# Last stage of an eight-sequence decoder: memory attention in chunks of 128 tokens with a carried state, one product for query and key, and the masked attention's shift per query by GpSimd and ScalarE

## What is computed

```
# memory attention (x: 8 x 512 x 256; M = 64; decay one number, 0.9 to 0.999)
q = x @ Wq; k = x @ Wk; v = x @ Wv; gates = sigmoid(x @ Wg + bg)
S = decay * S + (k_t*g_t)[:, None] * (v_t*g_t)[None, :]     # for t = 0, 1, ...
out_t = q_t @ S                                             # uses the new S
x = layernorm(x + (outs @ Wo + bo))
# masked attention to the context c
Q = x @ Wq.T + bq; K = c @ Wk.T + bk; V = c @ Wv.T + bv
attn = softmax(where(mask, -1e9, Q @ K.T))
x = layernorm(x + ((attn @ V) @ Wo.T + bo))
# experts: x @ expert_w[e] + expert_b[e], e = 0..7, weighted by thresholded softmax gates
```

## Time and profile before

| | |
|---|---|
| time, median of 3 runs | 2000.97 us (1998.99 to 2003.04) |
| the profiled execution's own time, its span | 1999.51 us, 1997.6 us |
| busy over the span: PE, PEld, DVE, ACT, POOL | 1829.3, 1077.1, 1250.3, 976.7, 614.7 us |
| mean granted TensorE clock, share of full speed | 0.970 |
| last stage | from 1377.6 us to the end |
| instructions | 26201 |

### The profile page before, as it was taken

How to read it: one execution, slowest core, us unless ns; L and a number is a source line. 1 busy time by engine, 2 the same in 40 slices (tenths; PEclk the granted TensorE clock), 3 DMA queues, 4 the chain that set the end, 5 groups by cost and what they waited for, 6 DMA issues and landing times. The chain is left out here.

```text
span 1997.6 us, 26201 instructions
## 1 busy us (share of the span) xinstructions
PE 1829.3 (92%) x8441; PEld 1077.1 (54%) x8441; DVE 1250.3 (63%) x2929; ACT 976.7 (49%) x2532; POOL 614.7 (31%) x795
## 2 busy tenths in 40 slices
PE   7999778899889888898879999998799999999997
PEld 5556434455444454454455566564466566556553
DVE  2686468888999989897302211322666776865665
ACT  4336599988989899895221111111233232222220
POOL 2010065555766666675400001002421212301100
PEclk9999989999999999999989999998889999999999
DMA  5348721122223122124633434423211111100000
GB/s 211 103 148 296 246 71 54 49 67 61 77 67 91 61 83 80 54 90 154 207 116 124 140 106 140 145 95 116 79 54 48 48 32 38 48 11 16 11 11 21
DMA packets 163800, 183.24 MB, mean 92 GB/s; under 512 B 19380, under 2 KB 143531, under 8 KB 162640
## 3 DMA queue, kind: packets, MB, share of 16 engines
q1 hardware_dynamic: 157520, 165.39, 25.9%
q0 software_dynamic: 6144, 16.18, 2.6%
HBM read 118.95 MB, written 63.18 MB: 91 GB/s over the span
## 5 line engine op out<-in xcount | busy, mean ns | idle before, releaser
L907 POOL TENSOR_SCALAR xa_probs<-xa_probs,xa_small 128x512 f32<-128x512 f32 x512 | 344.8, 690 | 244.8 <-DVE xa_small L1064 244.8
L973 ACT ACTIVATE xa_probs<-xa_ps_s,xa_small 128x512 f32<-128x512 f32 x512 | 361.1, 742 | 40.0 <-DVE xa_small L1070 36.1
L1070 DVE TENSOR_REDUCE xa_small<-xa_ps_s 128x2 f32<-128x1024 f32 x256 | 309.2, 1208 | 43.6 <-PE xa_ps_s L1341 43.6
L1354 PE MATMUL xa_ps_t<-xa_ident,xa_probs 128*128 128x128 f32 x2048 | 309.2, 284 | 17.0 <-DVE early L738 7.1
L1354 PEld LDWEIGHTS xa_ps_t<-xa_ident,xa_probs 128*128 128x128 f32 x2048 | 230.1, 143 | 153.3 <-ACT early L740 46.2
L2409 PE MATMUL ta_ps_e<-late,ta_x5T 128*128 128x512 f32 x512 | 236.9, 597 | 1.8 <-DVE ta_acc L2159 1.7
L1341 PE MATMUL xa_ps_s<-xa_k,xa_q 96*128 96x512 bf16 x496 | 152.3, 389 | 53.9 <-ACT xa_probs L973 53.9
L2159 DVE SCALAR_TENSOR_TENSOR ta_acc<-ta_ps_e,ta_gate,ta_acc 128x256 f32<-128x256 f32 x256 | 123.5, 482 | 95.0 <-PE ta_ps_e L2409 88.6
L1605 ACT ACTIVATE ex_hid<-ex_ps_g 128x512 f32<-128x512 f32 x64 | 38.2, 597 | 274.1 <-PE ex_ps_u L1702 274.1
L1656 DVE TENSOR_TENSOR ex_hid<-ex_hid,ex_ps_u 128x512 f32<-128x512 f32 x64 | 44.0, 688 | 185.1 <-ACT ex_hid L1605 185.1
L2409 PEld LDWEIGHTS ta_ps_e<-late,ta_x5T 128*128 128x128 f32 x512 | 96.4, 193 | 100.1 <-issue 83.7
(11 more groups left out here) (355 smaller groups left out, 3042.7 us busy)
## 6 DMA issues: line engine op xcount, KB each, us to landing
scratch_qk_parts<-front_w_all SPq DMA_DIRECT2D x16, 768.0 KB, 5.7
xa_q<-scratch_qk_parts SPq DMA_DIRECT2D x186, 64.0 KB, 2.3
xa_k<-scratch_qk_parts SPq DMA_DIRECT2D x186, 64.0 KB, 2.3
scratch_buf<-late SPq DMA_DIRECT2D x8, 1024.0 KB, 5.3
early<-in_L_ffn_Wg SPq DMA_DIRECT2D x16, 512.0 KB, 6.2
early<-in_L_ffn_Wu SPq DMA_DIRECT2D x16, 512.0 KB, 6.5
early<-in_L_ffn_Wd SPq DMA_DIRECT2D x16, 512.0 KB, 6.9
ex_xs<-scratch_buf SPq DMA_DIRECT2D x16, 512.0 KB, 5.2
```

The source lines that it names most:

```text
L907: ins = pool.tensor_scalar(probs[n % NP][:, t, :], probs[n % NP][:, t, :], rinv[n % 2][:, t:t + 1], 1.0, ALU.mult, ALU.mult)
L973: ins = act.activation(probs[n % NP][:, t, :], ps_s[j][:, t % 2, :], ACT.Exp, bias=nmax[n % 2][:, t:t + 1], accum_out=rsum[n % 2][:, t:t + 1])
L1070: dve.tensor_reduce(nmax[n % 2][:, 2 * j:2 * j + 2], ps_s[j][:, :, :], AX.X, ALU.max, negate=True).then_inc(max_up, 1)
L1354: ins = pe.transpose(ps_t[t % 2][:, i * P:(i + 1) * P], probs[m % NP][:, i, t * P:(t + 1) * P], ident[:, :])
```

## The change

**Memory attention.** The tokens are cut into four chunks of 128. Inside a chunk, scores and reading stay as they were (`m_scores`: four products of 128 columns into one buffer, `ps_a`; `m_faded`: one VectorE instruction of 512 columns). What earlier chunks leave is a 64 x 64 state: ScalarE makes `aged` (the keys times the decay to the end of the chunk, natural layout, 3 chunks), `m_outer` on TensorE multiplies it with the gated values, `m_carry` on VectorE chains the three states (state = whole * state + new), GpSimd makes `risen` (the queries times the decay since the chunk's start), and `m_reading` adds state times risen to the chunks 1 to 3. Query and key come from one product with the weights side by side (`m_qk`, 64 + 64 columns) in place of two padded ones, and the keys in natural layout come with the values (`m_vk`, 130 columns in place of 66 for three of the four tiles).

**Shift per query.** TensorE's `x_side` goes. GpSimd multiplies x4 by `cq_w`, now a row of 256 repeated over the partitions (`side`), and ScalarE sums each of the 4 tiles in an activation with an accumulator (`x_sides`).

**Stages before.** Fewer zero fills, one more weight load, one more small copy on GpSimd; the decay tables grow to 128 columns twice (`fade`, `rise`) in place of 512 once.

```diff
@@ gpsimd, stage_tail
                 if has(s_ - 1):
                     pool.wait_ge(m_x4, s_)
+                    wait(pool, x_cq, s_ - 1)
+                    pool.tensor_tensor(side[:, :, :], x4[(s_ - 1) % 2][:, :, :], row(cq_w[:, :]).to_broadcast([P, T, D]), ALU.mult).then_inc(x_side, 1)
                     wait(pool, x_z, T * (s_ - 1))
                     pool.tensor_tensor(x4b[:, :, :], ...).then_inc(m_x4b, 1)
+                if has(s_):
+                    pool.wait_ge(m_copy, 2 * s_ + 1)
+                    wait(pool, m_o, s_)
+                    pool.tensor_tensor(risen[:, :, :], qT[:, P:S].rearrange("p (t q) -> p t q", q=P),
+                                       row(rise[0:M, :]).to_broadcast([M, T - 1, P]), ALU.mult).then_inc(m_risen, 1)
@@ scalar
+                wait(act, m_kv, b)
+                act.activation(aged[:, :, :], ps_mkeys, ACT.Copy, scale=last).then_inc(m_aged, 1)
...
-            def x_side(b):
-                act.wait_ge(x_q, b + 1)
+            def x_sides(b):
+                act.wait_ge(x_side, b + 1)
+                for t in range(T):
+                    ins = act.activation(side[:, t, :], side[:, t, :], ACT.Copy, accum_out=cq_sum[:, t:t + 1])
+                ins.then_inc(x_sum, 1)
                 wait(act, x_ss, T * b)
-                act.activation(cq[:, :], ps_v[:, :, 0], ACT.Identity, bias=cq_b[:, 0:1]).then_inc(x_cq, 1)
+                act.wait_ge(x_sum, b + 1)
+                act.activation(cq[:, :], cq_sum[:, :], ACT.Identity, bias=cq_b[:, 0:1]).then_inc(x_cq, 1)
@@ vector
-            def m_faded(b, j):
-                dve.wait_ge(m_a, 4 * b + j + 1)
-                if j < 2:
-                    wait(dve, m_o, b)
-                else:
-                    dve.wait_ge(m_free, 2 * b + j - 1)
-                dve.tensor_tensor(aT[j % 2][:, 0:S - j * P], ps_s[j % 2][:, 0:S - j * P], fade[:, 0:S - j * P], ALU.mult).then_inc(m_at, 1)
+            def m_faded(b):
+                dve.wait_ge(m_a, b + 1)
+                wait(dve, m_o, b)
+                dve.tensor_tensor(aT[:, :, :], ps_a, row(fade[:, :]).to_broadcast([P, T, P]), ALU.mult).then_inc(m_at, 1)
+
+            def m_carry(b):
+                dve.wait_ge(m_kv, b + 1)
+                wait(dve, m_o, b)
+                dve.tensor_copy(state[:, 0, :], ps_kv[:, 0, :]).then_inc(m_state, 1)
+                for j in range(1, T - 1):
+                    dve.wait_ge(m_state, (T - 1) * b + j)
+                    dve.scalar_tensor_tensor(state[:, j, :], state[:, j - 1, :], whole[0:M, 0:1], ps_kv[:, j, :], ALU.mult, ALU.add).then_inc(m_state, 1)
@@ tensor
-                for n, w in enumerate((m_wq, m_wk)):
-                    for h in range(DH):
-                        ins = pe.matmul(ps_s[n][:, :], w[:, h, :], x3T[:, h, :], start=(h == 0), stop=(h == DH - 1))
-                    ins.then_inc(m_q, 1)
+                wait(pe, m_state, (T - 1) * b)
+                for h in range(DH):
+                    ins = pe.matmul(ps_s[0][:, :], m_qk[:, h, :], x3T[:, h, :], start=(h == 0), stop=(h == DH - 1))
+                ins.then_inc(m_q, 1)
...
+            def m_outer(b):
+                pe.wait_ge(m_aged, b + 1)
+                pe.wait_ge(m_gv, b + 1)
+                for t in range(T - 1):
+                    ins = pe.matmul(ps_kv[:, t, :], aged[:, t, :], gv[:, t, :], start=True, stop=True)
+                ins.then_inc(m_kv, 1)
+
+            def m_reading(b):
+                pe.wait_ge(m_at, b + 1)
+                pe.wait_ge(m_state, (T - 1) * (b + 1))
+                pe.wait_ge(m_risen, b + 1)
+                wait(pe, x_vs, 2 * b)
+                for t in range(T):
+                    ins = pe.matmul(ps_o[0:M, t * P:(t + 1) * P], gv[:, t, :], aT[:, t, :], start=True, stop=(t == 0))
+                    if t > 0:
+                        ins = pe.matmul(ps_o[0:M, t * P:(t + 1) * P], state[:, t - 1, :], risen[:, t - 1, :], start=False, stop=True)
+                ins.then_inc(m_o, 1)
...
-            def x_side(b):
-                wait(pe, m_gv, min(b + 2, B))
-                wait(pe, x_eT, T * b)
-                for t in range(T):
-                    for h in range(DH):
-                        ins = pe.matmul(ps_v[:, t, 0:2], x4T[:, h, t * P:(t + 1) * P], cq_w[:, h, :], start=(h == 0), stop=(h == DH - 1))
-                ins.then_inc(x_q, 1)
```

More of the change, by code:

```diff
@@ L582 @@
 M = 64
+W = 2 * M + 2
 MASKED = -1.0e9
@@ L602, in __init__ @@
         self.bq, self.bk, self.bv = (sb([P, DH]) for _ in range(3))
-        self.bqw, self.bvw = sb([P, DH, P]), sb([P, DH, P])
-        self.g_bias, self.cq_w, self.cq_b = sb([P, DH]), sb([P, DH, 2]), sb([P, 1])
+        self.bqw, self.bkw, self.bvw = (sb([P, DH, P]) for _ in range(3))
+        self.g_bias, self.cq_w, self.cq_b = sb([P, DH]), sb([P, D]), sb([P, 1])
         self.v_bias, self.bo = sb([P, D]), sb([P, D])
@@ L1646, in grow @@
                     dve.wait_ge(fade_up, 1)
-                wait(dve, grown, 2 * n)
-                dve.tensor_tensor(decay[:, n + 1:n + 2], decay[:, n:n + 1], decay[:, n:n + 1], ALU.mult).then_inc(grown, 1)
-                dve.tensor_scalar(k.fade[:, 1 << n:2 << n], k.fade[:, 0:1 << n], decay[:, n:n + 1], None, ALU.mult).then_inc(grown, 1)
+                    dve.wait_ge(decay_up, 2)
+                wait(dve, grown, 3 * n)
+                square = decay[:, n + 1:n + 2] if n + 1 < FADE else k.whole[:, :]
+                dve.tensor_tensor(square, decay[:, n:n + 1], decay[:, n:n + 1], ALU.mult).then_inc(grown, 1)
+                for row_ in (k.fade, k.rise):
+                    dve.tensor_scalar(row_[:, 1 << n:2 << n], row_[:, 0:1 << n], decay[:, n:n + 1], None, ALU.mult).then_inc(grown, 1)
             dve.wait_ge(sig_up, 1)
-            dve.tensor_scalar(decay[:, 0:1], sg[:, :], 0.999 - 0.9, 0.9, ALU.mult, ALU.add).then_inc(decay_up, 1)
+            for first in (decay[:, 0:1], k.rise[:, 0:1]):
+                dve.tensor_scalar(first, sg[:, :], 0.999 - 0.9, 0.9, ALU.mult, ALU.add).then_inc(decay_up, 1)
             for m in range(NU):
@@ L1753, in stage_tail @@
         z, z2 = r.sb("z", [P, T, D]), r.sb("z2", [P, T, D])
-        qT, kT, oT = (r.sb(n, [P, S]) for n in ("qT", "kT", "oT"))
+        qT, kT, oT = (r.sb(n, [M, S]) for n in ("qT", "kT", "oT"))
+        risen, state = r.sb("risen", [M, T - 1, P]), r.sb("state", [M, T - 1, M])
+        aged = r.sb("aged", [P, T - 1, M])
         g, g2 = r.sb("g", [P, T]), r.sb("g2", [P, T])
-        aT = [r.sb(f"aT{j}", [P, S]) for j in range(2)]
+        aT = r.sb("aT", [P, T, P])
         x4 = [r.sb(f"x4{u}", [P, T, D]) for u in range(2)]
@@ L1790, in stage_tail @@
         ps_o = r.ps("ps_o", [P, S])
+        line = ps_v[:, :, :].rearrange("p t q -> p (t q)")
+        ps_mv = [line[:, W * t:W * t + (W if t < T - 1 else M + 2)] for t in range(T)]
+        ps_mvalues = bass.AP(tensor=line.tensor, offset=0, ap=[[T * P, P], [W, T], [1, M]])
+        ps_mgates = line[:, M:M + W * (T - 1) + 1:W]
+        ps_mkeys = line[:, 0:W * (T - 1)].rearrange("p (t w) -> p t w", w=W)[:, :, M + 2:W]
+        ps_a = ps_s[1][:, :].rearrange("p (t q) -> p t q", q=P)
+        ps_kv = ps_s[0][0:M, 0:(T - 1) * M].rearrange("p (t m) -> p t m", m=M)
         ps_vx = ps_o[:, :].rearrange("p (t d) -> p t d", d=D)
@@ L1926, in x_turned @@
                 wait(act, x_g, b)
-                wait(act, x_q, b)
                 act.activation(x4T[:, :, :], ps_w[:, :, :], ACT.Copy).then_inc(x_xT, 1)
@@ L1984, in step @@
                 if has(b):
-                    x_side(b)
+                    x_sides(b)
                 if has(s_):
```

126 lines of the change are left out of this document (53 added, 73 removed).

## The result

The changed kernel takes 1976.29 us (median of four runs, 1975.09 to 1982.4) against 2002.01 us of the kernel before (four runs, 1998.99 to 2004.08): a ratio of 0.9886, 95% interval 0.9864 to 0.9907. It is faster, by 25.7 us between the medians and 24.2 us between the spans of the two profiled executions, and not by the 38 that I forecast; the time lies above my range, whose end was 1974.

What follows compares the result with a forecast made beforehand. The prediction took TensorE to bound the kernel. Its terms, −33.5 us in five full steps, −3 in steps 0 to 2 and −1.7 in step 8, made −38 from 2001.0, so 1963 us, range 1952 to 1974.

Steps and rivals of the forecast that it cites:

- 8 instructions for scores and 14 for readings at 0.108, 2.38 us: Full step, TensorE: with `m_outer` at 0.5 us these replace 5.97 us of scores and readings, −3.1 us a step.
- the floor of 0.108 us per instruction: TensorE: an instruction of up to 128 columns costs 0.108 us, read from products of 66 columns.
- Sum. −33.5: Steps 3 to 7: TensorE's savings of 6.7 us a step, over five full steps.
- my 64.9: Full step after the change: predicted length in us, so query and key products of steps 3 and 5 about 130 apart.
- the lower bound: Full step, six `m_outer` products: 0.32 us if load and columns both scale, half the upper bound of 0.65.
- Project, values, shift: Full step, TensorE: query and key in one product −1.72 us, values unchanged, `x_side` gone −1.89.
- The clock: Full steps: half clock behind the logits given back, 1.67 us a step; rival that it still falls: 1971 us, chance 0.16.
- The other engines in a full step: Full step: VectorE keeps 2.1 us of room, ScalarE's added work stays hidden with about 1 us; cost 0.
- Steps 0 to 2: First steps, chain over VectorE: 0 net for steps 0 and 1, −3 us for step 2.
- the sign of being wrong that I had named: Profile after: steps 0 to 2 longer than the 151 us they had by more than 2.
- one round fewer between TensorE and VectorE: Step 0: the carry needs one round where fadings 2 and 3 needed two, about 3 us, taken as 2.5.
- Step 8: Last step: `x_side` goes, 1.8 us there, taken as −1.7 us.

Runs made afterwards that it cites:

- full_tiles: Changed kernel with all memory-attention products padded by zeros to 128 rows and columns: 1967.54 us, ratio 0.984 to the kernel before.
- grouped: Changed kernel with the readings reordered, the four 128-row products first, then the three with the states: 1975.11 us, ratio 0.9887 to the kernel before.
- x_only: Kernel before with only the shift per query moved to GpSimd and ScalarE, memory attention as before: 1980.83 us, ratio 0.9915.
- m_only: Changed kernel with the shift per query back on TensorE as eight narrow products: 2010.31 us, ratio 1.0041 to the kernel before.
- gather_early: Changed kernel with GpSimd's gathers for the third batch right behind `risen` in step 0: 1978.31 us, ratio 0.9883 to the kernel before.
- late_mix: Changed kernel with VectorE combining the next batch behind the carry in steps 0 and 1: 1976.38 us, ratio 0.9881 to the kernel before.
- pool_later: Changed kernel with GpSimd doing `risen` first, then `side`, x3b and x4b once the next batch is combined: 1974.82 us, ratio 0.9885 to the kernel before.

## Why the prediction was wrong, point by point

**The step that failed** is "8 instructions for scores and 14 for readings at 0.108, 2.38 us", with the floor of 0.108 us per instruction taken to hold for any rows and columns, and "Sum. −33.5" from it. Measured: scores 1.09, readings 2.38, together 3.47 us, 1.1 more, and the neighbours that I had not counted: four units beside narrow products at 0.1 to 0.2 each, the output product 0.19, the transposition ahead of the scores 0.10, the logits 0.08: together 2.0 us a step, 4.66 for 6.7. Over five full steps that is 9.8 of the 14 us that are missing. full_tiles and grouped show the cause; full_tiles, whose step of 65.2 is near my 64.9, shows that the rest of the sum held. The trace of the kernel before had it (PE's timeline in step 4):
```profile
1631.12 0.60 PE L2394 MATMUL ta_ps_w<-late,ta_gate 128*8 128x128 f32 x4
1631.56 1.88 PE L2409 MATMUL ta_ps_e<-late,ta_x5T 128*128 128x512 f32 x4
1633.28 1.88 PE L2354 MATMUL ta_ps_s<-ta_cT,ta_gT 128*128 128x512 f32 x4
1635.09 1.99 PE L2400 MATMUL ta_ps_w<-late,ta_gateT 8*128 8x256 f32 x8
1637.01 1.98 PE L2354 MATMUL ta_ps_s<-ta_cT,ta_gT 128*128 128x512 f32 x4
1638.83 3.60 PE L2409 MATMUL ta_ps_e<-late,ta_x5T 128*128 128x512 f32 x8
```
The gate-bias product with 8 rows took 1.92 us for eight of 256 columns, where other eights of 256 take 1.73, and the products of 512 columns around it 1.81 and 1.82 for 1.72. I had not looked at products with few rows. One change costs nothing here, and in the same way after the change and in full_tiles: the transposition of the gates, with 128 rows and 8 columns (1631.12 to 1631.56, 0.44 us for four, and 1.72 for the unit behind it). Its load starts 0.18 us ahead of its product, as between equal shapes. Why it is spared, no run shows.

The Trainium skill (TensorE: Matmul & The Clock Gate, section "LDWEIGHTS (loading the stationary operand)") says that a load's time goes with its columns and not with its rows. The traces agree: the eight loads of the scores took 0.96 us with 64 rows and 0.97 with 128, the six of the outer products 0.42 with 64 columns and 0.75 with 128. What a change between neighbours costs doesn't follow from it. The outer products themselves took 0.49 us, my estimate 0.5, not the 0.32 of the lower bound.

Two slips of the prediction change nothing: the products of steps 3 and 5 start 143.17 us apart by their rows, and the 32 "products" ahead of the half clock are instructions, 16 products. After the change those of steps 3 and 5 start 133.86 us apart, not 130.

**Project, values, shift**: 1.72, 1.73 and 1.89 us, right. **The clock**: given back in steps 3 to 7, right in size (x_only: 1.57 us beside the shift's own 1.89), and for the reason that I gave, the shorter stretch of narrow products: it comes back with `x_side` gone and the old readings kept (x_only), and not with the new readings and `x_side` kept (m_only).

**The other engines in a full step**: right. The norm took 7.02 us, there is no gap around `m_outer` or the reading, and ScalarE's sums ended at 1615.9, ahead of the reading's end at 1617.65.

**Steps 0 to 2**: predicted −3, measured +2.8, the second term that failed and the sign of being wrong that I had named. Step 0 gained 2.7 where I said 2.5, but that is luck. My reason was one round fewer between TensorE and VectorE; x_only, with the old rounds, has 29.65 us, and of the eleven kernels with the new order seven have 32 us or more. What differed in these two executions is that x3b held VectorE's combining in the kernel before (4.37 us for 1.67), while after the change nothing held VectorE ahead of the outer products. Step 1 lost 6.1 where I had netted at 2.5 lost: I had added `side` to the time for which GpSimd's products hold VectorE, but one VectorE operation was held through three products back to back (a maximum of 6.06 us for an operation of 0.48, against 3.135 in the earlier trace rows), and behind it stood the gate's square. gather_early, late_mix and pool_later each take 3.8 to 6.6 us off step 1 by another edit, so the late rows, VectorE's order and GpSimd's hold are all needed for the wait. Step 2 gave 0.6 and not 3: GpSimd's products held the norm for 7.8 us, and the half clock stayed (0.50 from 1478 to 1493). x_only gave 4.1 there, and its norm was held almost as long, 7.48 us; but its clock was 1.00 over the same stretch. That points to the clock and not to GpSimd's hold, between two kernels that differ in the whole memory attention.

**Step 8** and step 7: 6.7, of it about 4.7 for step 7 and 2 for step 8; predicted 6.7 and 1.7. From 38 to the 24 between the profiled executions: 9.8 less in the five full steps, 5.8 less in steps 0 to 2, 1.3 more ahead of the stage and 0.3 more in step 8.

What stays open: what the half clock alone costs in steps 0 to 2, what ScalarE's sigmoid waits for in step 0 of some executions, and why the transposition with 8 columns costs no change.

## What to carry to other kernels

Price a product on TensorE with its neighbours: where a tile uses 64 of 128 rows or columns between full ones, try zeros for the rest, or put products of one shape together; in the full steps here zeros gave 1.7 us of 67. Look for products with few rows in the trace before the change; here the price stood there already. When two parts of a change both touch a stretch at half clock, test them alone: one of them may carry all of it, and the other be worth little without it. And where GpSimd gets a new long product, look for the small VectorE operations that read and write SBUF alone and stand on the way, not only for the large ones.
